# A four-layer attention kernel on one core: the first layer's loop on seven PSUM banks, with a subtraction moved to GpSimd and half of the maxima rows to ScalarE

## What is computed

```python
tokens = x.reshape(B, C, N).transpose(0, 2, 1)            # B 8, C 256, N 1024
qkv = (tokens @ w_proj + b_proj).reshape(B, N, 8, 96)
q, k, v = jnp.split(qkv, 3, axis=-1)                      # 32 each
attn = jax.nn.softmax(jnp.einsum('bihd,bjhd->bijh', q, k) * 32 ** -0.5, axis=2)
res = jnp.einsum('bijh,bjhd->bihd', attn, v).reshape(B, N, 256)
x = res @ w_out + b_out + tokens
```

## Time and profile before

| | us |
|---|---|
| three runs | 3104.37, 3099.82, 3094.11; median 3099.82 |
| the profiled execution | 3101.73 |
| its span, first to last instruction | 3100.0 |
| mean granted TensorE clock | 0.935 of full |

### The profile page before, as it was taken

How to read it: one execution, slowest core, us unless ns; L and a number is a source line. 1 busy time by engine, 2 the same in 40 slices (tenths; PEclk the granted TensorE clock), 3 DMA queues, 4 the chain that set the end, 5 groups by cost and what they waited for, 6 DMA issues and landing times.

```text
span 3100.0 us, 42243 instructions
## 1 busy us (share of the span) xinstructions
PE 2708.6 (87%) x14966; PEld 1854.5 (60%) x14966; DVE 2196.4 (71%) x2490; ACT 1220.1 (39%) x1348; POOL 603.8 (19%) x381
## 2 busy tenths in 40 slices
PE   5989979899898898988889888898888899888993
PEld 4447754577545775467754677447764477644772
DVE  4876678766687676867678576785678766787666
ACT  2443325433254333543335333353334533245334
POOL 0520116002160022500224002330024200242011
PEclk8999989999799998999989999899999999899996
DMA  6100050000500005000040001400022000310016
GB/s 154 27 25 1 1 130 1 25 1 14 117 1 25 1 14 117 1 25 1 21 110 1 25 1 38 93 7 19 1 69 62 25 1 1 94 37 25 1 55 244
DMA packets 46388, 124.57 MB, mean 40 GB/s; under 512 B 9792, under 2 KB 21312, under 8 KB 42560
## 3 DMA queue, kind: packets, MB, share of 16 engines
q1 hardware_dynamic: 46144, 121.41, 14.4%
HBM read 43.01 MB, written 23.86 MB: 22 GB/s over the span
## 4 chain that ended last, share of the span: by engine, by line
PE 69%; DVE 10%; ACT 8%; issue 6%; SPq 4%; DMA 3%; DVEq 0%; ACTq 0%
PE tile L1270 23%; PE pv L1270 10%; PE pv L1374 7%; PE tile L1364 6%; PE tile L1342 5%; ACT p L666 4%; PE tile L1515 4%; SPq L452 3%; PE tile L1394 3%; DMA stack<-qk_r 2%; DVE small L877 2%; PE tile L1537 2%; PE tile L1645 2%; PE tile L1564 1%; PE tile L1416 1%
## 5 line engine op out<-in xcount | busy, mean ns | idle before, releaser
L877 DVE TENSOR_REDUCE small<-tile 128x1 f32<-128x1024 f32 x512 | 612.6, 1220 | 125.0 <-PE tile L1342 121.1
L666 ACT ACTIVATE p<-tile 128x1024 f32<-128x1024 f32 x512 | 506.7, 1026 | 457.9 <-PE tile L1364 393.4
L1342 PE MATMUL tile<-stack 96*128 96x512 f32 x1024 | 356.9, 441 | 63.6 <-DMA stack<-qk_r 30.3
L1364 PE MATMUL tile<-stack 112*128 112x512 f32 x1024 | 369.0, 452 | 20.8 <-DVE small L877 14.1
L1270 PE MATMUL tile<-qk_r 128*128 128x512 f32 x1536 | 377.9, 395 | 0.0
L578 POOL TENSOR_TENSOR row_sum<-act 128x256 f32<-128x256 f32 x32 | 42.1, 1335 | 1640.0 <-DVE act L1105 1640.0
L553 POOL TENSOR_TENSOR acc<-acc,p 128x1024 f32<-128x1024 f32 x144 | 344.8, 2416 | 31.2 <-DVE acc L909 29.3
L1270 PEld LDWEIGHTS tile<-qk_r 128*128 128x128 f32 x1536 | 287.1, 188 | 66.4 <-issue 7.7
L1110 DVE TENSOR_TENSOR pl<-p,ph 128x1024 fp32r<-128x1024 f32 x128 | 158.2, 1236 | 238.0 <-ACT p L751 238.0
L1364 PEld LDWEIGHTS tile<-stack 112*128 112x128 f32 x1024 | 175.2, 196 | 241.7 <-issue 85.0
L1342 PEld LDWEIGHTS tile<-stack 96*128 96x128 f32 x1024 | 185.9, 202 | 187.2 <-ACT p L666 110.8
(11 more groups left out here) (277 smaller groups left out, 4256.0 us busy)
## 6 DMA issues: line engine op xcount, KB each, us to landing
stack<-qk_r SPq DMA_DIRECT2D x192, 256.0 KB, 5.0
x_in<-in_x_dram SPq DMA_DIRECT2D x9, 1024.0 KB, 7.6
act<-in_x_dram SPq DMA_DIRECT2D x8, 1024.0 KB, 8.0
x_scratch<-act SPq DMA_DIRECT2D x7, 1024.0 KB, 4.0
z_scratch<-zbuf SPq DMA_DIRECT2D x7, 1024.0 KB, 5.1
stack<-ones SPq DMA_DIRECT2D x8, 512.0 KB, 7.6
w3f<-w3f_scratch SPq DMA_DIRECT2D x8, 512.0 KB, 3.2
fin_rest<-z_scratch SPq DMA_DIRECT2D x3, 1024.0 KB, 12.7
```

Source lines behind the costliest of these rows:

```text
L666: sc.activation(p0[:, jt % DEPTH, pair, :], tile_wait(b, "st0", *u, jt, pair), ACT.Exp, scale=float(D) ** -0.5).then_inc(scalar_done, scal ...
L877: ve.tensor_reduce(maxima[:, h * NT + it:h * NT + it + 1], t[:], X, ALU.max).then_inc(vector_done, vector.one("max0", g, h, it))
L1342: ins = mm(o[:, s], stack[0:IMAX, 0, g, h, it * P:(it + 1) * P], stack[0:IMAX, 1, g, h, s], start=True, stop=True)
L1364: ins = mm(o[:, halves[k]], stack[0:K0, 1, g, h, jt * P:(jt + 1) * P], stack[0:K0, 0, g, h, halves[half]], start=True, stop=True)
```

## The change

PSUM in the first layer's loop is dealt out in another way. For all units but the last, and from the first unit's maxima on:

- `s0`, `m0`, `den0` and the first two `ex0` take turns on two whole tiles (ring "rows").
- `st0` is made for one head at a time, one bank each, on three banks in turn (ring "scores"): the two of the third tile, and that bank of `pv` which the running half of the queries doesn't use. `exp0` becomes four instructions of 512 columns a key tile. An `st0` of key tile 0 in the `pv` bank waits for `pv0_out`, ScalarE's copy of the last unit's sum.
- the order within a key tile becomes `s0`, `st0`, `st0`, `s0`, `st0`, `st0`, `pv0`.
- everything else ("whole"), the last unit with its pairs of heads included, goes on taking turns on three tiles, by a count of its own. By that count the last unit's first `st0` gets the tile in which `den0` of the unit before lies.

Of the rows of negated maxima, VectorE now writes those of heads 0 and 1; those of heads 2 and 3 are written by ScalarE in four instructions of 16x256 (`max_cols`), at the head of each unit's list, before its exponentials and, in the first unit, behind the wait for the DMAs. The transposes of `m0` are laid so that each engine reads its own bank.

`res_lo` goes from VectorE to GpSimd for the first three units, put in behind its two adds of key tile 1. The value bias is taken out of `res_hi` and `res_lo` and folded with `w_out` once, in the setup, into the output bias (`bvo0`): four matmuls of one column and one small add.

```diff
+def key_tile(g, half):
+    if next_unit(g, half):
+        return ("s0", 0), ("st0", 0), ("st0", 1), ("s0", 1), ("st0", 2), ("st0", 3)
+    return ("st0", 0), ("st0", 1)
...
 def pool_steps():
-    s = [("add0", *u, jt, pair) for u in UNITS for jt in range(NT) for pair in range(2)
-         if adder(*u, jt, pair) == "pool"]
+    s = []
+    for u in UNITS:
+        for jt in range(1, SUMMED):
+            s += [("add0", *u, jt, pair) for pair in range(2) if adder(*u, jt, pair) == "pool"]
+            s += [("res_lo", *last_unit(*u))] if last_unit(*u) and jt == 1 else []
...
+    home, rings = {}, {"whole": 0, "rows": 0, "scores": 0}
+    for n in tiles:
+        kind, unit, looped = n[0], n[1:3], False
+        if kind in ("st0", "den0"):
+            looped = unit != UNITS[-1]
+        elif kind == "s0":
+            looped = n[3] // HT + n[1] > 0
+        elif kind == "m0":
+            looped = unit != UNITS[0]
+        elif kind == "ex0":
+            looped = next_unit(*unit) not in (None, UNITS[-1])
+        ring = ("scores" if kind == "st0" else "rows") if looped else "whole"
+        if ring == "scores":
+            home[n] = ((2, 0), (2, 1), (3, 1 - n[2]))[rings[ring] % 3]
+        else:
+            home[n] = (rings[ring] % (2 if ring == "rows" else SLOTS), None)
+        rings[ring] += 1
...
+                        if jt == 1 and last_unit(*u):
+                            g, half = last_unit(*u)
+                            cols_ = slice(half * HALF, (half + 1) * HALF)
+                            pool.wait_ge(scalar_done, scalar.at(b, "res_hi", g, half))
+                            pe.tensor_tensor(side[:, 1, g, cols_], raw[:, cols_], side[:, 0, g, cols_].bitcast(F32),
+                                             ALU.subtract).then_inc(pool_done, gps.one("res_lo", g, half))
...
+                def max_cols(g, half):
+
+                    m = tile_wait(b, "m0", g, half)[0:NMAX, HALF:HALF + G // 2 * P].rearrange("p (h n) -> p h n", n=P)
+                    for t in range(HT):
+                        it = HT * half + t
+                        sc.activation(stack[IMAX:K0, 0, g, G // 2:G, it * P:(it + 1) * P], m, ID, scale=mask8[:, it:it + 1]
+                                      ).then_inc(scalar_done, scalar.one("max_cols", g, half, t))
...
                 for u in UNITS:
                     last = last_unit(*u)
+                    if last:
+                        pv0_out(*last)
+                    max_cols(*u)
                     for jt in range(NT):
-                        if last and jt == 0:
-                            pv0_out(*last)
-                        for pair in range(2):
-                            exp0(u, jt, pair)
+                        for k in range(score_tiles(*u)):
+                            exp0(u, jt, k)
```

More of the change, by code:

```diff
@@ L115, in scalar_steps @@
     for u in UNITS:
+        s += [("pv0_out", *last_unit(*u))] if last_unit(*u) else []
+        s += [("max_cols", *u, t) for t in range(HT)]
         for jt in range(NT):
-            s += [("pv0_out", *last_unit(*u))] if last_unit(*u) and jt == 0 else []
-            s += [("exp0", *u, jt, pair) for pair in range(2)]
+            s += [("exp0", *u, jt, k) for k in range(score_tiles(*u))]
             s += [("res_hi", *last_unit(*u))] if last_unit(*u) and jt == 2 else []
@@ L149, in vector_steps @@
                 s += [("add0", *u, jt - 1, pair)] if jt and adder(*u, jt - 1, pair) == "vector" else []
-            s += [("res_lo", *last)] if last and jt == 3 else []
         if following:
             s += [(n, *following) for n in ("neg_hi", "neg_copy", "neg_lo")]
-            s += [("max_rows", *following, h) for h in range(G)]
+            s += [("max_rows", *following, h) for h in range(G // 2)]
     s += [("stat", 1, 0, ct) for ct in range(CT)]
@@ L244, in conv_seq_kernel, with banks, leavers @@
     place = {n: k for k, n in enumerate(tiles)}
-    def slot(*name):
-        return place[name] % SLOTS
-    def leaver(b, *name):
-        k = place[name]
-        former = tiles[k - SLOTS] if k >= SLOTS else [n for n in tiles if slot(*n) == k][-1]
-        engine, *step = last_reader(former)
-        steps = {"scalar": scalar, "vector": vector}[engine]
-        return engine, (steps.at if k >= SLOTS else steps.before)(b, *step)
+    home, rings = {}, {"whole": 0, "rows": 0, "scores": 0}
[15 more added lines that the diff above has]
+        rings[ring] += 1
+    def slot(*name):
+        assert home[name][1] is None
+        return home[name][0]
+    def banks(name):
+        k, half = home[name]
+        return [(k, q) for q in range(2) if half in (None, q)]
+    def leavers(b, *name):
+        k, found = place[name], {}
+        for bank in banks(name):
+            users = [n for n in tiles[k + 1:] + tiles[:k] if bank in banks(n)]
+            if bank[0] == SLOTS:
+                users = [n for n in tiles[:k] if bank in banks(n) and n[1:3] == name[1:3]]
+            for engine, *step in last_readers(users[-1]) if users else ():
+                steps = {"scalar": scalar, "vector": vector}[engine]
+                now = place[users[-1]] < k
+                found[engine] = max(found.get(engine, (False, 0, None)), (now, steps.place[tuple(step)], tuple(step)))
+        return [(engine, ({"scalar": scalar, "vector": vector}[engine].at if now
+                          else {"scalar": scalar, "vector": vector}[engine].before)(b, *step))
+                for engine, (now, _, step) in found.items()]
     x_v = x.rearrange("b (t p) h w -> b p t (h w)", p=P)
@@ L357, in conv_seq_kernel, with where @@
         pv = ctx.enter_context(nc.psum_tensor("pv", [P, N], F32))
+        def where(*name):
+            k, half = home[name]
+            t = (*tile, pv)[k]
+            return t[:] if half is None else t[:, half * HALF:(half + 1) * HALF]
         names = ["bq0", "bk0", "bv0", "bo0", "gnw", "gnb", "bq1", "bk1", "bv1", "bo1", "bq2", "bk2",
-                 "bv2", "bo2", "b3", "bnw", "bnb", "bvo1", "bvo2", "scale", "shift", "bnscale", "bnshift"]
+                 "bv2", "bo2", "b3", "bnw", "bnb", "bvo0", "bvo1", "bvo2", "scale", "shift", "bnscale", "bnshift"]
         def col(name, ct=None):
@@ L898, in add0 @@
                 def add0(u, jt, pair):
[L899 removed]
+                    scalar_wait(*exp_of(*u, jt, pair))
                     if u[0] == 1 and jt == 1:
@@ L991, in _ @@
                                 add0(u, jt - 1, pair)
-                        if last and jt == 3:
-                            res_lo(*last)
                     if following:
@@ L1321, in free @@
                 def free(*name):
-                    engine, count = leaver(b, *name)
-                    pe.wait_ge(scalar_done if engine == "scalar" else vector_done, count)
-                    return tile[slot(*name)]
+                    for engine, count in leavers(b, *name):
+                        pe.wait_ge(scalar_done if engine == "scalar" else vector_done, count)
+                    return where(*name)
                 kts = range(CT)
```

103 lines of the change are left out of this document (64 added, 39 removed).

## The result

The changed kernel takes 3151.85 us (median; 3145.87 to 3156.54), the kernel before 3102.1 beside it on the same chip: a ratio of 1.0164 (1.0137 to 1.0191), 50 us slower. The prediction was 3142. The profiled span went from 3100.0 to 3148.4.

The account below looks back on a forecast made before the run. GpSimd's chain of adds, with VectorE's, was taken to bound the units: 1.0 + 2 x 1.7 + 0.9 = 5.3 us a batch, 42 in eight, from 3101.7 to 3144, median 1.9 lower: 3142; 80% range 3080 to 3165.

Parts of the forecast that it names:

- likeliest case: Whole kernel: GpSimd's and VectorE's chain lengthens the units; 3142 us, own range 3120 to 3165, chance 62%.
- Middle units: Units (0,1) and (1,0): 34.85 us against 33.11, each 1.7 longer, through GpSimd's and VectorE's adds and `res_lo`.
- The chain: GpSimd's adds, `res_lo` and VectorE's adds in a middle unit, from M (transpose `m0` opening it) to M + 34.85.
- First unit: No `res_lo`, but `max_cols` behind ScalarE's wait for the last DMA of `stack`: 1.0 us longer.
- GpSimd's start: GpSimd's first add in the first unit, 463.71 before: 1.4 us later, from 1.8 of `max_cols` partly won back.
- Last unit: First `st0` gets the tile of `den0` and waits for `rec0`: 0.9 us longer.
- The sum: All units of a batch: 1.0 + 2 x 1.7 + 0.9 = 5.3 us longer, 42 in eight batches.
- TensorE's pauses: Middle units: TensorE pauses 2.6 us before key tile 6 and some 2.4 before the transpose.
- First rival: VectorE gets in first behind GpSimd's adds (2,1) and (4,1): 1.0 us less a batch, 3092 us; 18%.
- Third rival: TensorE's clock falls behind its new pauses: some 4 us a unit, two a batch, 3206 us; 7%.
- The rule on the shared ports: Where adds meet, whichever issues first blocks the other; GpSimd, needing no semaphore, goes first: 3142 us, otherwise 3092.
- The two rows: Kernel before: VectorE's add of 2.11 us and `res_lo` of 2.52, read as let in at GpSimd's end when already waiting.

Follow-up runs that it names:

- e4: Kernel before with `res_lo` on GpSimd behind its adds of key tile 1 and the value bias folded into the output bias: 3120 us, ratio 1.0075.
- e1: Changed kernel, but GpSimd's add (5,0) of key tile 5 waits for VectorE's add (5,1): 3122 us, ratio 1.0080.
- e2: Changed kernel with `res_lo` back on VectorE behind the adds of key tile 2: 3163 us, ratio 1.0215.
- e9: Changed kernel with ScalarE's four `max_cols` of the first unit ahead of its wait for the copies into `stack`: 3127 us, ratio 1.0093.
- e5: Changed kernel with the ring "rows" of two whole tiles starting one tile later: 3147 us, ratio 1.0163.
- e10: Changed kernel with the edits of e1, e5 and e9 together: 3083 us, ratio 0.9945 to the kernel before.
- e11: e10, with GpSimd's add of key tile 3 waiting for VectorE's as well: 3128 us, ratio 1.0087.
- e3: Changed kernel, but in the first unit VectorE writes the maxima rows of all four heads: 3128 us, ratio 1.0100.
- e8: Changed kernel with `res_lo` and all maxima rows back on VectorE, leaving the banks alone: 3120 us, ratio 1.0079.
- e6: Kernel before, with GpSimd's add of key tile 5 made to wait for VectorE's: 3100 us, ratio 1.0008.
- e7: Changed kernel with the edits of e1, e2, e3 and e5 together: 3104 us, ratio 1.0034.

## Why the prediction was right, point by point

It was right in sign and 0.3% low in size, with its own likeliest case. That it came so near is in part luck: two of its terms were off in opposite directions, the two middle units 0.9 a batch too long together and the first unit 1.5 too short (some 8 us too much and 12 too little in eight batches).

- **Middle units**: predicted +1.7 each, measured +1.28 and +1.19 (second batch, as below). The chain holds step by step: start M + 8.46 (8.5), wait for `res_hi` 0.96 (1.0), `res_lo` 1.28 (1.28), VectorE's adds 3.40 and 3.38 (3.4), the second ending at M + 31.5 (31.9), transpose 2.9 behind (3.0). The last six adds took 15.03 with the hold-up in them, not 15.3. e4 confirms that `res_lo` on GpSimd lengthens these units by 1.2, e1 (at full clock) that GpSimd's add going first at key tile 5 makes 2.1 us of the unit. The reverse of e4 fails: with the new banks, `res_lo` back on VectorE (e2) gives 0.6 and 0.5, since it is late there.
- **First unit**: predicted +1.0, measured +2.65 (2.5 on the mean). The step that failed is GpSimd's start, taken 1.4 later, measured 3.4 (M + 12.55; before, M + 9.19, 463.71). The four `max_cols` themselves took less than thought, 1.53 for 1.8. But the prediction counted only their length behind the wait for the copies. Before, TensorE had used that wait for its first `st0` and `s0`; now it stood through it, since heads 2 and 3 need `max_cols`, and since the first `s0` takes the tile that holds the maxima. e9 shows it: the same operations ahead of the wait cost nothing.
- **Last unit**: predicted +0.9, measured +0.90. e5 and e10, with the ring turned by one, take 1.2 off.
- **The sum**: 5.3 predicted per batch, 5.9 measured on the mean of eight.
- **TensorE's pauses**: 2.6 predicted before key tile 6, 1.84 measured, key tiles being 3.08 apart and not 2.98 (478.42, 481.50, 484.57 in the first unit). Of the 2.4 predicted before the transpose 0.68 was left; TensorE was later there, 3.4 us of it at 1.2 GHz behind the first pause.
- **First rival** (VectorE gets in first): refuted by the 3.40 and 3.38. e1 makes it so by force at key tile 5: 32.3 us at full clock where it had said 32.7, but 33.3 on the mean.
- **Third rival** (the clock falls, 7%): the price was wrong in kind. The clock did fall, mean 0.95 in both middle units, but behind the pause before key tile 6, where the adders' chain covered it. It was set at 7% on one pause of 2.93 us with full speed behind it; one such row does not show that a pause is harmless. e11 is what the rival described, a fall at the seam: the whole kernel is 45 us slower than e10.
- **The rule on the shared ports.** Both contended adds show GpSimd first and VectorE behind it, as the prediction had it. The Trainium skill (SBUF - State Buffer, Who interferes with whom) says that whichever of the two issues first has the shared ports for its whole instruction and the other fully blocks. The runs agree that neither is slowed in part: VectorE's add ends 1.08 or 1.09 behind the end of the GpSimd add that it waited for. By the recorded starts they disagree on one point: an operation of VectorE that starts ahead of GpSimd's next add can still be passed over by it (last section). The two rows that the prediction had the earlier trace rows could not show this: behind the one GpSimd add its next waited for it, behind the other GpSimd's next waited for VectorE.

So by the units, the 50 us are some 20 in the first unit, some 20 in the two middle ones and 8 in the last. e4 has the middle ones with `res_lo` on GpSimd alone (20 us in its middle units, 23 in all), e9 and e3 undo the first (25 and 24 us), e5 and e10 the last. But the parts are not independent: e8 has neither `res_lo` on GpSimd nor `max_cols` and is still 24 over. The last unit's tile is in it (8 us), and its middle units are 0.6 and 0.7 longer than before, since VectorE's `res_lo` then is late instead.

## What to carry to other kernels

When work moves to an idle engine, look at the place in that engine's queue, not only at its busy share: four operations of 0.4 us were free ahead of a wait and cost 3.6 us behind it, and one `res_lo` of 1.28 us, with a wait of 0.96 before it, moved a unit by 1.2, since GpSimd's and VectorE's adds then set its end. Where VectorE and GpSimd both add into SBUF and one depends on the other, look whether they meet at all (in e6 they did not, and the order was worth nothing), and try a semaphore that decides who goes first at the last meeting: forced there it gave 26 us, forced at the meeting before it as well it cost 45 (e11 over e10). A pause that is due to a slower engine's chain does not vanish when its nearest cause is taken away; ask where it goes, and whether TensorE's clock is needed there.

## What the hardware showed that was not expected

- A waiting VectorE operation is not always let in at the end of GpSimd's add. In the kernel before, `res_lo` started 1.97 us before the end of (3,0) (506.06 to 508.03) and went next. In e2, e7 and e8, in each of the middle units, it started 1.2 to 1.4 us before the end of (2,1) (518.84 to 520.09) and had to sit out (3,0) too, 4.14 us in all.

The traces show a difference between the two ends. Add (3,0) waits for an add that has been done for over 2 us, and it starts 0.04 us before the recorded end of (2,1): no gap. Add (4,0) waits for (3,0), which GpSimd has only just done, and starts 0.08 us behind its end. In the kernel before, `res_lo` went in there, and (4,0) took 0.3 us longer than an add alone:

```profile
508.11 2.70 POOL L553 TENSOR_TENSOR acc<-acc,p 128x1024 f32<-128x1024 f32 x1
```

In the fourteen traces 415 operations of VectorE with two operands in SBUF were held up by over 0.25 us by GpSimd's adds of the first layer. All of them went in at an end behind which GpSimd's next instruction was at least 0.08 us away. All 48 `res_lo` that met an end without such a gap (e2, e7, e8) were passed over there. So the misses of e2 and e8 have their likely reason in which add `res_lo` meets. No run was aimed at this, and it is no general rule: behind the first layer, eight times in every kernel, a VectorE add (the first starts at 373.46 in the kernel before) went in at an end behind which GpSimd's next operation, of 256 columns, is recorded without a gap.

- The same pause of TensorE, 1.84 us, was followed by 1.2 GHz in one unit of e1 and by 2.4 GHz in the next. The kernel before has only pauses of up to 0.43 us inside its second unit and keeps 1.00 through both middle units. In e4 TensorE pauses 1.76 us before the transposes that end the middle units, and the clock stays at 1.00 there too. Behind 2.27 us before the transposes that end the first unit they take 0.60 in all eight batches of the kernel after, and 1.02 in four of eight in e5.
- ScalarE's operation on 16 x 256 elements with a scale operand takes 0.38 us each in a row of four (1.53).
- The rest of the batch, whose code hardly differs, took from 248 to 255 us, in different batches of one kernel too (247.9 to 254.6 in the kernel before), with a mean granted clock of 0.72 to 0.84 in the stretches shown.
